# Attention within each sequence's own block: scores and value mix in quarters of the array, softmax and transposes on half the columns

## The reference, cut to what matters

```python
b, s, _ = x.shape                     # 32, 64, 1024
qkv = x @ w_qkv.T + b_qkv
q, k, v = jnp.split(qkv, 3, axis=-1)  # 512 each: 8 heads of 64
scores = jnp.einsum('bhfc,bhtc->bhft', k, q)
scores = jnp.where(causal[None, None], scores, MASKED_BIAS)
attn = jax.nn.softmax(scores, axis=-2)
vals = jnp.einsum('bhft,bhfc->bhtc', attn, v)
out = vals @ w_o.T + b_o
```

## Time and profile before

| what | value |
|---|---|
| time, median of 3 runs | 1096.44 us (1095.72 to 1097.54) |
| the profiled execution's own time | 1096.46 us |
| its span | 1094.7 us |
| TensorE busy | 1013.5 us, 93% of the span |
| VectorE busy | 583.9 us, 53% |
| ScalarE busy | 459.9 us, 42% |
| GpSimd busy | 403.8 us, 37% |
| granted TensorE clock, mean | 0.975 of full speed |

### The profile page before, as it was taken

One profiled execution on the slowest core, in us unless ns is written; L12 is line 12 of the kernel. 1 busy time (PEld: TensorE's weight loads), 2 busy tenths in 40 slices (PEclk: granted clock), 3 DMA queues, 4 the chain that ended last, 5 costly groups with the idle time before them and its releaser, 6 DMA issues.

```text
span 1094.7 us, 13928 instructions
## 1 busy us (share of the span) xinstructions
PE 1013.5 (93%) x5084; PEld 783.8 (72%) x5084; DVE 583.9 (53%) x864; ACT 459.9 (42%) x757; POOL 403.8 (37%) x323
## 2 busy tenths in 40 slices
PE   7999999997998999997899999999999889888886
PEld 6877777785877888875688788888887767433332
DVE  6253534586357214436773484485174567966561
ACT  6245354544435424433342342352142232576663
POOL 2224333057303025424332332430023378757422
PEclk9999999998999999999999999999999989899998
DMA  8654562775163164254002002000214775444411
...
DMA packets 71563, 133.04 MB, mean 122 GB/s; under 512 B 29255, under 2 KB 30279, under 8 KB 66894
## 3 DMA queue, kind: packets, MB, share of 16 engines
...
## 4 chain that ended last, share of the span: by engine, by line
PE 54%; issue 10%; POOL 7%; DVE 5%; DMA 3%; ACT 2%; POOLq 0%; SPq 0%; DVEq 0%; ACTq 0%
PE bank L308 12%; PE bank L310 12%; PE bank L309 12%; PE bank L1845 4%; PE bank L1744 3%; PE bank L1855 3%; POOL vacc L344 2%; PE bank L1599 2%; PE bank L1722 1%; DVE sq L386 1%; ACT gt L1103 1%; PE bank L1734 1%; DMA stage<-w_qkv_t 1%; POOL hg L762 1%; DVE acc L1248 1%
## 5 line engine op out<-in xcount | busy, mean ns | idle before, releaser
L344 POOL TENSOR_TENSOR vacc<-vacc,sq 128x512 f32<-128x512 f32 x72 | 97.4, 1352 | 46.8 <-ACT sq L390 37.9
L308 PE MATMUL bank<-xa_h,wp_h 128*128 128x512 f32 x256 | 103.1, 403 | 6.6 <-DVE xa_l L1125 6.6
L308 PE MATMUL bank<-cv_h,wf_h 128*128 128x512 f32 x256 | 105.5, 412 | 1.9 <-POOL wf_l L302 1.9
L310 PE MATMUL bank<-cv_h,wf_l 128*128 128x512 f32 x256 | 101.3, 396 | 0.0
L309 PE MATMUL bank<-xa_l,wp_h 128*128 128x512 f32 x256 | 100.9, 394 | 0.0
L309 PE MATMUL bank<-cv_l,wf_h 128*128 128x512 f32 x256 | 100.8, 394 | 0.0
L310 PE MATMUL bank<-xa_h,wp_l 128*128 128x512 f32 x256 | 100.7, 393 | 0.0
L710 POOL TENSOR_TENSOR fo<-fo,res 128x512 f32<-128x512 f32 x32 | 43.7, 1375 | 129.0 <-ACT fo L849 91.9
L1103 ACT ACTIVATE gt<-bank 128x512 f32<-128x512 f32 x128 | 66.1, 600 | 22.4 <-PE bank L1855 22.2
L390 ACT ACTIVATE sq<-sq 128x512 f32<-128x512 f32 x56 | 35.1, 632 | 70.4 <-DVE sq L386 70.4
L1855 PE MATMUL bank<-gt,dn_f 128*64 128x512 f32 x256 | 63.5, 614 | 0.0
...
## 6 DMA issues: line engine op xcount, KB each, us to landing
...
```

The lines of the kernel that those rows point to most:

```text
L308: pe.matmul(o, wh, xh, start=start, stop=False)
L310: return pe.matmul(o, wl, xh, start=False, stop=stop)
L344: g.tensor_tensor(vacc[:, :], t[:, 0, :] if k == 1 else vacc[:, :], t[:, k % 2, :], ALU.add).then_inc(ln_pool, 1)
```

## The change

Scores are now computed for each sequence of a tile alone: `c_scores` makes 16 f32 matmuls of 64 rows, 64 x 64 outputs, in place of 8 of 128 x 128. Head j chooses the half of the array's rows (partitions of `qk`) and the bank, and the tile's parity i chooses the half of the output partitions, so that two tiles lie on top of each other in 128 partitions, and a bank holds 256 columns in place of 512. Softmax, exp, `pr` and `pt` shrink to 256 columns per head. `c_turn` makes 4 transposes, both heads into one bank. `c_mix` makes 16 matmuls of 64 x 64 for both heads at once, head j choosing the output partitions and sequence s the rows and the bank (7 and 3). ACT alone copies `pt` (one copy of 512 columns), and evacuates the values in two instructions of 128 x 256 in place of two of 64 x 512. DVE's `c_pt` is gone (so are its calls). The -3e38 mask for foreign sequences is gone. The loop over chunks 1 and 2 is written out. At the end the last turn follows the mix of pair 2 at once, and the last mix stands before the groups `(0, 1, 2)` and `(0, 1, 3)` instead of behind them.

```diff
@@ -132,8 +131,8 @@
         xc_h = place("xc_h", [P, KB, N], F32R, E)
         xc_l = place("xc_l", [P, KB, N], F32R, E + 16 * KIB)
         qk = place("qk", [P, 2, N], F32, E + 32 * KIB)
-        pr = place("pr", [P, 2, N], F32, E + 40 * KIB)
-        pt = place("pt", [P, 2, N], F32, E + 44 * KIB)
+        pr = place("pr", [P, 2, N // 2], F32, E + 40 * KIB)
+        pt = place("pt", [P, 2, N // 2], F32, E + 44 * KIB)
         vo = place("vo", [P, N], F32, E + 52 * KIB)
 
         wo_h = place("wo_h", [P, PAIRS, D], F32R, R2)
...
@@ -214,10 +213,8 @@
 
         def chunks(e, first, last, body):
 
-            body(first)
-            if last - first > 1:
-                with e.Fori(first + 1, last) as c:
-                    body(c)
+            for c in range(first, last):
+                body(c)
 
         def released(e, c, k, blocks, used, done):
...
@@ -665,26 +662,24 @@
-            for t, value in ((ident, 0.0), (mean_w, 1.0 / D), (eps, EPS), (valid, 1.0), (maskf, 1.0), (negs, OTHER), (fold, 0.0)):
+            for t, value in ((ident, 0.0), (mean_w, 1.0 / D), (eps, EPS), (valid, 1.0), (maskf, 1.0), (negs, MASKED), (fold, 0.0)):
-                g.affine_select(out=maskf[part, part], in_=maskf[part, part], compare_op=ALU.is_gt, fill=0.0,
+                g.affine_select(out=maskf[part, :], in_=maskf[part, :], compare_op=ALU.is_gt, fill=0.0,
                                 base=0, pattern=[[1, SEQ]], channel_multiplier=-1).then_inc(masks_ok, 1)
-                g.memset(negs[part, part], MASKED).then_inc(masks_ok, 1)
...
@@ -987,19 +982,18 @@
                 act.activation(qk[:, 0, :], bank[0][:, :], ACT.Identity,
                                bias=vec[:, B_Q + m:B_Q + m + 1]).then_inc(q_ev, 1)
 
-            def c_pt(c, m, banks=PT_BANK):
-                since(act, pt_mm, c, 8, 2 * m + 1)
-                since(act, pv_mm, c, 8, 2 * m - 1)
-                act.activation(pt[:, 0, :], bank[banks[0]][:, :], ACT.Copy).then_inc(pt0_ev, 1)
-
-            def c_vals(c, m):
-                for j in range(2):
-                    rowsj = slice(HEAD * j, HEAD * j + HEAD)
-                    since(act, pv_mm, c, 8, 2 * m + j + 1)
-                    if j == 0:
-                        since(act, vo_st, c, 64, 16 * m)
-                    act.activation(vo[rowsj, :], bank[7][rowsj, :], ACT.Identity,
-                                   bias=vec[rowsj, B_V + m:B_V + m + 1]).then_inc(vo_ev, 1)
+            def c_pt(c, m, b=PT_BANK):
+                since(act, pt_mm, c, PAIRS, m + 1)
+                since(act, pv_mm, c, PAIRS, m)
+                act.activation(pt[:, :, :], bank[b][:, :].rearrange("p (j n) -> p j n", j=2), ACT.Copy).then_inc(pt_ev, 1)
+
+            def c_vals(c, m, banks=PV_BANK):
+                since(act, pv_mm, c, PAIRS, m + 1)
+                since(act, vo_st, c, 64, 16 * m)
+                for s in range(2):
+                    act.activation(vo[:, :].rearrange("p (t s q) -> p s t q", s=2, q=SEQ)[:, s],
+                                   bank[banks[s]][:, 0:N // 2].rearrange("p (t q) -> p t q", q=SEQ), ACT.Identity,
+                                   bias=vec[:, B_V + m:B_V + m + 1]).then_inc(vo_ev, 1)
 
             for u in range(U_V, U_V + 16):
                 unit_hi(act, u)
...
@@ -1300,19 +1294,18 @@
             def c_softmax_in(c, m):
                 for j in range(2):
                     i = 2 * m + j + 1
-                    S = bank[4 + j]
-                    view = S[:, :].rearrange("p (t n) -> p t n", t=TILES)
+                    view = bank[4 + j][:, 0:N // 2].rearrange("p (t n) -> p t n", t=TILES)
                     since(v, s_mm, c, 8, i)
 
                     v.memset(smax[:, j, :], 0.0)
-                    v.copy_predicated(view, masked[:, :].unsqueeze(1).to_broadcast([P, TILES, P]),
-                                      negs[:, :].unsqueeze(1).to_broadcast([P, TILES, P])).then_inc(s_masked, 1)
+                    v.copy_predicated(view, masked[:, :].unsqueeze(1).to_broadcast([P, TILES, SEQ]),
+                                      negs[:, :].unsqueeze(1).to_broadcast([P, TILES, SEQ])).then_inc(s_masked, 1)
                     since(v, s_masked, c, 8, i)
                     v.tensor_reduce(smax[:, j, :], view, AX.X, ALU.max).then_inc(s_max, 1)
                     since(v, s_max, c, 8, i)
-                    since(v, pt_mm, c, 8, i - 2)
+                    since(v, pt_mm, c, PAIRS, m)
                     v.tensor_tensor(pr[:, j, :].rearrange("p (t n) -> p t n", t=TILES), view,
-                                    smax[:, j, :].unsqueeze(2).to_broadcast([P, TILES, P]),
+                                    smax[:, j, :].unsqueeze(2).to_broadcast([P, TILES, SEQ]),
                                     ALU.subtract).then_inc(s_sub, 1)
 
             def c_softmax_out(c, m):
...
@@ -1324,13 +1317,8 @@
                     since(v, s_sum, c, 8, i)
                     v.reciprocal(ssum[:, j, :], ssum[:, j, :]).then_inc(s_rec, 1)
                     since(v, s_rec, c, 8, i)
-                    v.tensor_tensor(view, view, ssum[:, j, :].unsqueeze(2).to_broadcast([P, TILES, P]),
+                    v.tensor_tensor(view, view, ssum[:, j, :].unsqueeze(2).to_broadcast([P, TILES, SEQ]),
                                     ALU.mult).then_inc(s_norm, 1)
-
-            def c_pt(c, m, banks=PT_BANK):
-                since(v, pt_mm, c, 8, 2 * m + 2)
-                since(v, pv_mm, c, 8, 2 * m)
-                v.tensor_copy(pt[:, 1, :], bank[banks[1]][:, :]).then_inc(pt1_ev, 1)
 
             c_center(0)
             c_scale_first()
...
@@ -1715,35 +1699,43 @@
                 since(pe, q_ev, c, 4, m + 1)
                 since(pe, k_ev, c, 4, m + 1)
                 since(pe, s_sub, c, 8, 2 * m)
-                heads = [slice(HEAD * j, HEAD * j + HEAD) for j in range(2)]
-                for t in range(TILES):
-                    cols = slice(t * P, (t + 1) * P)
-                    for j, r in enumerate(heads):
-                        mm = pe.matmul(bank[4 + j][:, cols], qk[r, 0, cols], qk[r, 1, cols], start=True, stop=True)
-                        if t == TILES - 1:
-                            mm.then_inc(s_mm, 1)
-
-            def c_turn(c, m, banks=PT_BANK):
+                halves = [slice(HEAD * j, HEAD * j + HEAD) for j in range(2)]
+                for u in range(TILES // 2):
+                    for s in range(2):
+                        for i in range(2):
+                            at = (2 * u + i) * P + s * SEQ
+                            for j in range(2):
+                                mm = pe.matmul(bank[4 + j][halves[i], u * P + s * SEQ:u * P + (s + 1) * SEQ],
+                                               qk[halves[j], 0, at:at + SEQ], qk[halves[j], 1, at:at + SEQ],
+                                               start=True, stop=True)
+                                if (u, s, i) == (1, 1, 1):
+                                    mm.then_inc(s_mm, 1)
+
+            def c_turn(c, m, b=PT_BANK):
                 for j in range(2):
                     since(pe, s_norm, c, 8, 2 * m + j + 1)
+                    if j == 0:
+                        since(pe, pt_ev, c, 4, m)
                     if m == 0 and j == 0:
                         since(pe, v_ev, c, 4, 4)
-                    since(pe, (pt0_ev, pt1_ev)[j], c, 4, m)
-                    for t in range(TILES):
-                        cols = slice(t * P, (t + 1) * P)
-                        mm = pe.transpose(bank[banks[j]][:, cols], pr[:, j, cols], ident[:, :])
-                    mm.then_inc(pt_mm, 1)
-
-            def c_mix(c, m, js=(0, 1)):
-                for j in js:
-                    since(pe, (pt0_ev, pt1_ev)[j], c, 4, m + 1)
-                    since(pe, vo_ev, c, 8, 2 * m + j)
-                    since(pe, v_ev, c, 4, 4)
-                    for t in range(TILES):
-                        cols = slice(t * P, (t + 1) * P)
-                        mm = pe.matmul(bank[7][:, cols], vv[:, t, m * P:(m + 1) * P], pt[:, j, cols],
-                                       start=True, stop=True)
-                    mm.then_inc(pv_mm, 1)
+                    for u in range(TILES // 2):
+                        at = j * N // 2 + u * P
+                        mm = pe.transpose(bank[b][:, at:at + P], pr[:, j, u * P:(u + 1) * P], ident[:, :])
+                mm.then_inc(pt_mm, 1)
+
+            def c_mix(c, m, banks=PV_BANK):
+                since(pe, pt_ev, c, 4, m + 1)
+                since(pe, vo_ev, c, 8, 2 * m)
+                since(pe, v_ev, c, 4, 4)
+                halves = [slice(HEAD * j, HEAD * j + HEAD) for j in range(2)]
+                for t in range(TILES):
+                    for j in range(2):
+                        col = m * P + j * HEAD
+                        for s in range(2):
+                            mm = pe.matmul(bank[banks[s]][halves[j], t * SEQ:(t + 1) * SEQ],
```

(32 more changed lines are left out.)

47 lines of the change are left out of this document (20 added, 27 removed).

## The result

| kernel | median, us | beside it, before | ratio, 95% interval |
|---|---|---|---|
| changed | 1062.18 (1062.03 to 1063.88, 4 runs) | 1096.99 (4 runs) | 0.9689 [0.9665, 0.9712] |
| changed, again | 1068.25 (1062.09 to 1070.53, 6 runs) | 1104.08 (11 runs) | 0.9658 [0.9627, 0.969] |

The change makes the kernel 3.1% faster, 34 us. The forecast of 1070 us (1057 to 1084) holds the time, but 8 us of gain were left out of it. The second row was measured later, on another occasion, and there the kernel before was slower too, so the ratios are what can be compared. The profiled execution took 1062.28 us; its span is 1060.5.

The account below looks back on a forecast made before the run. The prediction took TensorE, busy 93% of the span, as the bound. Gains of 11.5 + 5.3 + 1.8 + 6.3 + 1.7 = 26.6 us took 1096.46 us to 1070 us, range 1057 to 1084.

Parts of the forecast that it names:

- rival 1: Scores and mix calls: all four array quarters overlap, 0.5 us a call, 10.9 us more gain, 1059 us; chance 0.2.
- New scores and new mix: 32 records of 64 columns each: Scores and mix calls: two records at a time at 56 ns, 0.89 us a call.
- the clock term: Behind the idle at `o_group(1, 0, 0)`: the low clock goes with that idle, gaining 1.7 us.
- Rivals 2 and 3: Per call: 2, issue pace bounds, 1.25 us, total 1080, chance 0.18; 3, slower records, 1.98 us, total 1100, chance 0.06.
- Pair 1: Pair 1 of each chunk: scores wait for k, so the shorter turn gains 0 us.
- takes up whatever is gained before it: Chunk 0, within qk(2): TensorE's 5.1 us wait for POOL absorbs gains behind the first scores; 0 us.
- Seven groups: Pair 2 of four chunks, pair 0 of chunks 1 to 3: 4.10 us becomes 2.42, counted 1.65 each, 11.5 us.
- The mixes inside the value projection: Pair 3's mix, three times: two mixes of 0.89 become one, 0.6 us each, 1.8 us gained.
- Pair 3: Pair 3 of all chunks: 5.3 us gained, despite a newly exposed 1 us wait for k in chunks 0 to 2.
- The end of chunk 3: First output projection to `o_group(1, 0, 0)`: 31.6 us becomes about 25, `vs` load and TensorE arriving together; 6.3 us gained.
- Rival 4: Output stage: gain at chunk 3's end given back where VectorE, POOL and DMAs bound; 8 us less, 1078 us; chance 0.1.
- Halving the softmax buys nothing by itself: Whole kernel: TensorE is busy 93% of the span, VectorE 53%, so only TensorE's time and waits count.

Follow-up runs that it names:

- rows_only: Changed kernel with scores and mix matmuls reordered so neighbours differ only in the row half: 1071.38 us, ratio 0.9736 to the kernel before.
- cols_only: Changed kernel with scores and mix matmuls reordered so neighbours differ only in the column half: 1071.04 us, ratio 0.9733 to the kernel before.
- one_by_one: Changed kernel with each quarter's scores and mix matmuls issued one after the other: 1083.63 us, ratio 0.9847 to the kernel before.
- turn_twice: Changed kernel with each transpose issued twice, so a turn has 8 records again: 1066.02 us, ratio 0.9702 to the kernel before.
- k_first: Changed kernel with q and k of pair 3 evacuated ahead of the eighth xc block: 1060.86 us, ratio 0.9658 to the kernel before.
- before_no_loop: Kernel before with only its loop over chunks 1 and 2 written out: 1098.58 us, ratio 0.9992 to the kernel before.
- mix_last: Changed kernel with the last mix moved back behind two projection steps: 1064.93 us, ratio 0.9690 to the kernel before.
- the long softmax: Changed kernel with each row maximum taken three times and each row sum twice: 1071.99 us, ratio 0.9760 to the kernel before.

## Why the prediction was right, and where it was not

The time lies in the stated range because the range took in rival 1 as well; it lies outside the 1066 to 1074 us of the forecast proper.

**The size of a call failed.** The step "New scores and new mix: 32 records of 64 columns each", with "I take 0.89 us", is the mis-sized term. A call takes 0.52 us. The lower bound had it: four records in the time of one, 0.45, "call it 0.5". What the forecast took for likeliest, two at a time, is what `rows_only` and `cols_only` do, and these cost 5 us, not 10. A call of two at a time is shorter than 0.89 us too: turn, mix and scores together take 2.02 us (`rows_only`, 708.81 to 710.83) where the forecast had 2.42, because the second half of the array starts before the first is done. The 0.2 us of entering and leaving were right: from the turn to the mix 0.53 us where four transposes take 0.44, and from the scores to the projection 0.62 where a call takes 0.52.

**Rival 1 was the mechanism.** The four quarters do overlap, and `one_by_one`, which has the same amount of work, shows that this makes about half of the gain (17 of 34 us). Read record by record, the mix at 704.86 starts four records, one in each quarter, 6 to 7 ns apart, and the next four 58 ns behind them; 58 ns is also what `one_by_one` shows for one quarter. The Trainium skill, TensorE: Matmul & The Clock Gate, Part 3, says that row and column tiles compose, with about 4 ns between starts of different tiles; the trace agrees that they compose, with 64-column streams too, and shows 6 to 7 ns. By the rival's figure the time was 1059; the 3 us to 1062.28 are the start-up (1.3 late in this profile), the slower clock in chunk 0 (1.0) and 0.6 that the output stage gave less than the clock term. Rivals 2 and 3 fall with the same rows: records of different quarters start 6 to 7 ns apart, 16 on average, so 39 ns is no pace of issue. The Trainium skill, TensorEngine Tiling (Array Packing), Instruction Overhead, which has about 60 cycles for each matmul, and the Trainium skill, TensorE: Matmul & The Clock Gate, Back-to-back issue gap, which has 62 ns per MATMUL when the sequencer issues them, do not bound this shape in this trace; in which of its two ways the records are issued here, no run shows.

**Pair 1: "no gain" is wrong by 0.47 us a chunk.** The argument about the turn holds (0.45 us of waiting, `turn_twice` in pair 1 costs nothing). The gain is from the scores call; the first scores of chunk 0, for which the sum had no term, gave as much. That POOL's wait in chunk 0 "takes up whatever is gained before it" is wrong as well. From the first scores to the var matmul it takes 25.1 us where it took 26.0, with the same wait. ScalarE's squares follow its copy of `pt`, and so the turn, so POOL's chain starts earlier with it; and POOL's first sum takes 1.29 us where it took 1.71, for which no run shows the reason.

**Seven groups** gave 16.8 for 11.5, all of it from the call.

**The mixes inside the value projection** gave 3.0 for 1.8, likewise.

**Pair 3** gave 7.0 for 5.3, again by the call; the newly exposed wait was there with its cause, size (1.15 to 1.23 for "1 us") and instant (2.37 for 2.4). `k_first` takes most of it away, which shows the cause.

**The end of chunk 3**: 25.0 us for 25.1, and only 0.19 us of idle at `o_group(1, 0, 0)`. The load and TensorE arrive together within 0.19 us.

**The clock term** was right in its place and incomplete. The low clock behind `o_group(1, 0, 0)` is gone, but the clock in the output stage falls elsewhere. Added up as above, the output stage loses 17.1 us to half speed before, 12.4 after, and 17.2 in the second profile of the same changed kernel.

**Rival 4**, the gain given back, is not seen at its size of 8 us, and a smaller part is not excluded. From `o_group(1, 0, 0)` to the end, the two profiles with the old order there (the kernel before and `before_no_loop`) take 243.1 and 241.2 us, and the eleven with the new order (all others but `mix_last`) 240.3 to 248.5, 243.6 on average. Less what half speed takes in each, it is 226.0 and 228.8 against 226.6 to 231.4, 229.1 on average. So by a rough estimate 1 to 2 of the 6.6 us are given back, within a scatter of 5; ten of the eleven also wait 4.04 us at the next `vs_l` (847.96 after) where before it is 2.64 (881.27). No run here holds the clock fixed.

**"Halving the softmax buys nothing by itself"** does not carry over to the changed kernel. With the long softmax the short matmuls lose 8 to 11 us of their gain. VectorE's share of 53% hid it, since what counts is VectorE's lateness at k, in pair 3 of chunks 0 to 2 and in pair 2 of chunk 3. What halving alone would do in the kernel before, no run shows.

**The loop** was worth nothing, as said.
